# Key-query products of a linear attention: float32 products replaced by three rounded products of a split

## The reference, cut to what matters

```
phi(x) = exp(x @ omega.T - max(x @ omega.T)) / sqrt(128) + 1e-6        (128 features; the term in |x|^2 cancels)
qp, kp = phi(heads(x @ Wq)), phi(heads(x @ Wk));  v = heads(x @ Wv)
out[s] = sum_{t<=s} (qp[s] . kp[t]) v[t]  /  (sum_{t<=s} (qp[s] . kp[t]) + 1e-6)
```

## Time and profile before

| | |
|---|---|
| runs, us | 849.5, 846.65, 847.43; median 847.43 |
| profiled execution, us | 851.56 |
| its span, us | 849.6 |
| TensorE's mean granted clock, share of full | 0.987 |
| TensorE busy, us | 812.2 (96%) |
| VectorE busy, us | 617.9 (73%) |
| ScalarE busy, us | 428.7 (50%) |
| GpSimd busy, us | 401.4 (47%) |

### The profile page before, as it was taken

How to read it: one execution, slowest core, us unless ns; L and a number is a source line. 1 busy time by engine, 2 the same in 40 slices (tenths; PEclk the granted TensorE clock), 3 DMA queues, 4 the chain that set the end, 5 groups by cost and what they waited for, 6 DMA issues and landing times.

```text
span 849.6 us, 21134 instructions
## 1 busy us (share of the span) xinstructions
PE 812.2 (96%) x5921; PEld 760.3 (89%) x5922; DVE 617.9 (73%) x1770; ACT 428.7 (50%) x1184; POOL 401.4 (47%) x567
## 2 busy tenths in 40 slices
PE   6889999999999999999999999999989899999995
PEld 5778999999999999999999999999887799999994
DVE  4536787878888788878888888887776566666663
ACT  4335627365462735446372645627142366666663
POOL 5320233534526353452636245263435348787675
PEclk9889999999999999999999999999999999999998
DMA  9635936557483654738375574836499457777780
GB/s 266 213 119 196 309 104 226 180 185 271 140 277 112 237 200 162 268 132 286 97 253 181 181 252 145 288 109 231 168 426 364 149 102 130 123 127 127 115 135 3
DMA packets 105673, 161.19 MB, mean 190 GB/s; under 512 B 10672, under 2 KB 69616, under 8 KB 104752
## 3 DMA queue, kind: packets, MB, share of 16 engines
q1 hardware_dynamic: 79616, 115.62, 41.1%
q0 software_dynamic: 15792, 35.17, 17.1%
q10 hardware_dynamic: 10224, 9.89, 4.4%
HBM read 50.14 MB, written 112.47 MB: 191 GB/s over the span
## 4 chain that ended last, share of the span: by engine, by line
PE 87%; DVE 5%; issue 2%; POOL 2%; DMA 1%; ACT 1%; SPq 0%; POOLq 0%; DVEq 0%; ACTq 0%
PE ps L791 74%; PE ps L802 5%; PE ps L1016 3%; PE ps L1114 2%; PE ps L1136 2%; POOL rstd L605 1%; DVE stat L1434 1%; DVE xn L1445 1%; DMA raw_wT<-in_omegaT 1%; POOL expert_rows L676 0%; POOL veps L603 0%; DVE mv L1438 0%; DMA expert_rows<-relu_v,place_i 0%; DVE kpT L1664 0%; DVE fT_lo L1452 0%
## 5 line engine op out<-in xcount | busy, mean ns | idle before, releaser
L782 POOL DMA_INDIRECT out<-narrow,sidx x79 | 122.4, 1550 | 50.6 <-DVE sidx L1825 27.6
L616 POOL CAST ctx_hi<-ctx_raw 128x512 fp32r<-128x512 f32 x16 | 10.2, 639 | 191.1 <-DMA ctx_raw<-in_ctxT 188.5
L791 PE MATMUL ps<-w_hi,fT_hi 128*128 128x256 f32 x256 | 79.3, 310 | 1.4 <-DVE fT_lo L1452 1.4
L1238 ACT ACTIVATE phi<-ps,nmax 128x128 f32<-128x128 f32 x256 | 73.0, 375 | 5.5 <-DVE nmax L1573 5.4
L791 PE MATMUL ps<-hT_hi,w_hi 128*128 128x256 f32 x256 | 73.1, 286 | 1.5 <-DVE hT_lo L1452 1.5
L1187 ACT ACTIVATE xn3T<-ps 128x512 f32<-128x512 f32 x17 | 10.2, 599 | 124.5 <-PE ps L802 124.5
L791 PE MATMUL ps<-hT_hi,w_lo 128*128 128x256 f32 x256 | 72.4, 283 | 0.0
L791 PE MATMUL ps<-hT_lo,w_hi 128*128 128x256 f32 x256 | 72.4, 283 | 0.0
L791 PE MATMUL ps<-w_hi,fT_lo 128*128 128x256 f32 x256 | 72.2, 282 | 0.0
L791 PE MATMUL ps<-w_lo,fT_hi 128*128 128x256 f32 x256 | 72.1, 282 | 0.0
L1252 ACT ACTIVATE relu_v<-ps,b_sb 128x256 f32<-128x256 f32 x128 | 67.0, 523 | 0.0
(11 more groups left out here) (300 smaller groups left out, 2866.5 us busy)
## 6 DMA issues: line engine op xcount, KB each, us to landing
expert_rows<-zero_rows SPq DMA_DIRECT2D x16, 4352.0 KB, 14.6
narrow<-expert_rows ACTq DMA_DIRECT2D x71, 136.0 KB
expert_up_hi<-X SPq DMA_DIRECT2D x16, 352.0 KB, 2.8
e_lo<-expert_up_lo POOLq DMA_DIRECT2D x2, 2816.0 KB, 13.9
e_hi<-expert_up_hi POOLq DMA_DIRECT2D x2, 2816.0 KB, 22.5
part_raw<-in_E SPq DMA_DIRECT2D x30, 176.0 KB, 2.8
expert_up_lo<-part_raw SPq DMA_DIRECT2D x15, 352.0 KB, 3.1
X<-in_x SPq DMA_DIRECT2D x16, 256.0 KB, 2.8
```

The source lines that it names most:

```text
L782: pool.indirect_dma_start(out_rows, bass.IndirectOffsetOnAxis(sidx[:, u:u + 1], 0), yg[:, u, :], None, bounds_check=NT * P - 1, oob_is_err ...
L791: return pe.matmul(out_, lhsT, rhs, start=start, stop=stop)
L1238: last = act.activation(phi[:, g, h, :], ps[:, g, h * M:(h + 1) * M], ACT.Exp, bias=nmax[:, g, h:h + 1])
```

## The change

Key and query features become pairs like the other matrices. ScalarE now writes the rounded parts of both, `qpT` and `kpT`, without the scale and with an added 1e-6 x sqrt(128). VectorE writes the remainders, `qpT_lo` and `kpT_lo`, with one instruction of 1024 columns each, from PSUM and the rounded part; they lie in the memory of `phi`, where each head's `aT` now has 512 columns, so that it overwrites its own head's remainders. TensorE does `mm3` for both products of a head: six rounded products in place of two float32 ones. The scale, twice 1/sqrt(128), lies in the mask's ones. VectorE waits for all of the turned keys and for both of ScalarE's halves of each.

```diff
@@ -64,6 +64,7 @@
     NASSIGN = NT * P * TOPK
     SCORE_SCALE = float(D) ** -0.5
     PHI_SCALE = float(M) ** -0.5
+    EXP_EPS = FEAT_EPS / PHI_SCALE
     PROJ_SCALE = float(DH) ** -0.25
     V1W = DH + 1
     ATW = S + P
@@ -184,9 +185,11 @@
         X = sb1("X", [P, NT, D])
         wq, wk = (cut(pair(n, DC * H * M), "p (c n) -> p c n", c=DC) for n in ("wq", "wk"))
         wv, wo = (cut(pair(n, DC * D), "p (c n) -> p c n", c=DC) for n in ("wv", "wo"))
-        phi = sb1("phi", [P, 4, H, M])
-        qpT = sb1("qpT", [P, H, S])
-        kpT = sb1("kpT", [P, H, S])
+        with ExitStack() as phi_scope:
+            phi = sb1("phi", [P, 4, H, M], F32, phi_scope)
+        pT_lo = sb1("pT_lo", [P, H, 2 * S], F32R)
+        qpT = sb1("qpT", [P, H, S], F32R)
+        kpT = sb1("kpT", [P, H, S], F32R)
         xnT, attnT = (cut(pair(n, DC * S), "p (c s) -> p c s", c=DC) for n in ("xnT", "attnT"))
         attn_cols = 2 * (2 * DC * H * M + 2 * DC * D) + 4 * H * M + 2 * H * S + 4 * DC * S
         up_cols = NE * 2 * INTER
@@ -231,7 +234,9 @@
         assert TS * TOPK * RW <= 4 * S + TS * H * V1W
         rows_cross = xn_attn[:, :].rearrange("p (t j w) -> p t j w", t=TS, j=TOPK)
         rows_last = relu_v1[:, 0:TS * TOPK * RW].rearrange("p (t j w) -> p t j w", t=TS, j=TOPK)
-        aT = phi[:, :, :, :].rearrange("p g h m -> p (g h m)")[:, 0:H * ATW].rearrange("p (h s) -> p h s", h=H)
+        of_head = phi[:, :, :, :].rearrange("p g h m -> p (g h m)").rearrange("p (h w) -> p h w", h=H)
+        aT = of_head[:, :, 0:ATW]
+        qpT_lo, kpT_lo = (pT_lo[:, :, n * S:(n + 1) * S] for n in range(2))
         early_scope.close()
 
 
@@ -569,9 +574,9 @@
             pool.memset(halfneg[:, :], -0.5).then_inc(const_ready, 1)
             pool.memset(eps_ln[:, :], LN_EPS).then_inc(const_ready, 1)
             pool.memset(eps_attn[:, :], ATTN_LN_EPS).then_inc(const_ready, 1)
-            pool.memset(feat_eps[:, :], FEAT_EPS).then_inc(const_ready, 1)
+            pool.memset(feat_eps[:, :], EXP_EPS).then_inc(const_ready, 1)
             pool.memset(v1[:, :, :, DH:V1W], 1.0).then_inc(const_ready, 1)
-            pool.memset(mask[:, :], 1.0).then_inc(blank, 1)
+            pool.memset(mask[:, :], PHI_SCALE * PHI_SCALE).then_inc(blank, 1)
             pool.wait_ge(blank, 2)
             pool.affine_select(out=ident[:, :], in_=ones[:, :], compare_op=ALU.is_equal, fill=0.0, base=0,
                                pattern=[[-1, P]], channel_multiplier=1).then_inc(const_ready, 1)
@@ -1032,11 +1037,13 @@
                 if last_cross:
                     count_choices()
                 if a is not None:
-                    pe.wait_ge(qpT_ready, a + 1)
-                    pe.wait_ge(kpT_ready, a + 1)
+                    pe.wait_ge(qpT_ready, (a + 1) * 2)
+                    pe.wait_ge(kpT_ready, (a + 1) * 2)
                     for h in range(H):
-                        mm(ps[:, h, 0:S], kpT[:, h, 0:P], qpT[:, h, :])
-                        mm(ps[:, h, S:ATW], kpT[:, h, P:S], qpT[:, h, P:S]).then_inc(aT_ps, 1)
+                        for cols_out, keys, lo in ((slice(0, S), slice(0, P), 0), (slice(S, ATW), slice(P, S), P)):
+                            last = mm3(ps[:, h, cols_out], (kpT, kpT_lo), (qpT, qpT_lo), (slice(None), h, keys),
+                                       (slice(None), h, slice(lo, S)), True, True)
+                        last.then_inc(aT_ps, 1)
                 if f is not None and not last_ffn:
                     ffn_out(1, 2, FC // 2)
                 if a is not None:
@@ -1330,8 +1337,12 @@
                 if a is not None:
                     for n in range(2):
                         act.wait_ge(qpT_ps, a * 2 + (n + 1))
-                        last = act.activation(qpT[:, 2 * n:2 * n + 2, :], bank(n), ACT.Identity,
-                                              bias=feat_eps[:, 0:1], scale=PHI_SCALE)
+                        last = act.activation(qpT[:, 2 * n:2 * n + 2, :], bank(n), ACT.Identity, bias=feat_eps[:, 0:1])
+                    last.then_inc(qpT_ready, 1)
+                    for n in range(2):
+                        act.wait_ge(kpT_ps, a * 2 + (n + 1))
+                        last = act.activation(kpT[:, 2 * n:2 * n + 2, :], bank(2 + n), ACT.Identity,
+                                              bias=feat_eps[:, 0:1])
                     last.then_inc(qpT_ready, 1)
                 for p in splits_of(i):
                     hold(act, part_loaded, (i + 1) * (4 * 16))
@@ -1659,11 +1670,12 @@
                     dve.wait_ge(egap_ready, r + 1)
                     gates(r)
                 if a is not None:
-                    for n in range(2):
-                        dve.wait_ge(kpT_ps, a * 2 + (n + 1))
-                        last = dve.tensor_scalar(kpT[:, 2 * n:2 * n + 2, :], bank(2 + n), PHI_SCALE, FEAT_EPS,
-                                                 ALU.mult, ALU.add)
-                    last.then_inc(kpT_ready, 1)
+                    dve.wait_ge(kpT_ps, (a + 1) * 2)
+                    for n, (lo, hi) in enumerate(((qpT_lo, qpT[:, :, :]), (kpT_lo, kpT[:, :, :]))):
+                        dve.wait_ge(qpT_ready, a * 2 + (n + 1))
+                        whole = ps[:, 2 * n:2 * n + 2, :].rearrange("p n (h s) -> p (n h) s", h=2)
+                        dve.scalar_tensor_tensor(lo, whole, EXP_EPS, hi.bitcast(F32), ALU.add, ALU.subtract)\
+                            .then_inc(kpT_ready, 1)
                 if nxt is not None:
                     hold(dve, x_loaded, (nxt + 1) * 16)
                     ln_stats(0, nxt, lambda t: x_tile(nxt, t))
```

## The result

The changed kernel takes 876.61 us (median of 4 runs, 874.49 to 877.54) against 847.04 of the kernel before in the same comparison; the ratio is 1.0343, with an interval of 1.0318 to 1.0367. The forecast was slower, 865.6 us, range 857 to 884: the direction and the range held, but the cost is 29.6 us and not 18.2.

The account below looks back on a forecast made before the run. TensorE, busy 812.2 of 849.6 us, was taken as the bound, with VectorE's chain to xn3 level in five turns. 5 x 1.15 + 8 x 1.0 + 1.5 + 1.8 + 1.15 = 18.2 us on 847.43 gave 865.6, range 857 to 884.

Parts of the forecast that it names:

- The step that failed: Turns 0 and 1: longer waits for the features plus 0.34 us for the products, 1.5 and 1.8 us.
- (a): Rival: short rounded products no cheaper than float32 ones, 213 ns at 128 columns, 880 us; chance 0.27.
- (d): Rival: VectorE's remainders at 1.64 us, 0.8 us more in each turn, 878 us; chance 0.10.
- Steady turns: Turns 2 to 14: VectorE's delay to xn3 adds 1.15 us in five turns and 1.0 in eight.
- The five turns that waited for `xn3`: Turns where TensorE already waited 0.5 us for VectorE's normalised rows; VectorE's delay adds its full 1.15 us.
- TensorE's late start: Key-query products in turn 8 start at 334.47, 0.52 us late, behind VectorE's remainders.
- The products: 24 rounded key-query products per turn at 0.12 us each: 2.88 us, 0.34 longer than now.
- (b): Rival: split stays under the cover, only TensorE's saving is left, 10 us less, 837 us; chance 0.06.
- The remainders: VectorE's one instruction of 1024 elements each for q and k: 1.25 us, pitch 1.17, upper end 1.64.
- ScalarE's: ScalarE also does the two kpT halves; the 1.17 us move is covered by idle time and costs nothing.
- The last turn: No successor to normalise: 0.8 us for the start and 0.34 for the products, 1.15 us.

Follow-up runs that it names:

- e1_warm01: Changed kernel with needless matmuls filling TensorE's waits of turns 0 and 1: 865.83 us, ratio 1.0225.
- e7_before_warm: Kernel before with needless matmuls in TensorE's waits of turn 0: 847.96 us, ratio 1.0007.
- e6_two_stages_warm: Changed kernel, waits of turns 0 and 1 filled, first two products of heads 0 and 1 ahead of the wait for the keys' remainder: 865.43 us, ratio 1.0158.
- e2_warm0: Changed kernel with needless matmuls filling TensorE's waits of turn 0 only: 871.36 us, ratio 1.0279.
- e5_split_only: Changed kernel with remainders written but unused, two plain float32 products per head on the rounded parts: 869.74 us, ratio 1.0223.
- e3_before_late01: Kernel before with needless VectorE reductions ahead of kpT in turns 0 (two) and 1 (three): 855.26 us, ratio 1.0096.
- e4_products_only: Changed kernel without remainders, rounded parts standing in for them in the three products, evictions as before: 849.43 us, ratio 0.9993.

## Why the prediction was right, and where it was not

- **The step that failed** is the one for turns 0 and 1, "1.15 + 0.34 = 1.5" and "1.8". They measured 7.1 and 6.8 us. What was missing is a term: the clock. Filling the waits (e1_warm01) takes 6.1 and 5.1 us back and leaves 1.0 and 1.7. The rows of before had a sign of it: behind the 1.86 us wait of turn 0 the 16 float32 records took 4.24 us, behind no wait 2.78, for the clock was at the lower level from 29.0 to 32.4 us. The prediction never looked at the granted clock by stretch. That this low stretch grows long when rounded products follow the wait could not be read from the trace of before.
- **The number.** The range held, but by luck: its upper part was there for rivals (a) and (d), 880 and 878, and neither happened. That e1_warm01's 865.83 us is the forecast's 865.6 is in part luck too: the steady turns cost 1.1 us more than forecast and the last turn 1.15 less. The 1.0 us of its turn 0 is against a kernel before whose own clock fell there; against e7_before_warm, filled like it, it is 2.8 us, with 1.5 forecast, and where the other 1.3 lie is open.
- **Steady turns.** Forecast 13.75 us for the turns 2 to 14, measured 11.8 in the two traces and 14.9 with the slow `rstd` taken out of both. An ordinary turn from 5 on grew by 1.08 us (36.88 to 37.96), with 1.0 forecast, and the mechanism was right: VectorE's chain and not TensorE's late start sets it (e6_two_stages_warm). The turns 2, 3 and 4 differ: like with like they grew by 0.7, 2.0 and 1.4. The five turns that waited for `xn3` were read as a property of those turns, where they are those in which `rstd` was slow in that execution. On VectorE the delay of 1.3 us at the mask products shrinks to 1.0 at the statistics, since the four mask products waited for heads before (2.27 us) and run on without a wait now (1.94). TensorE's own delay of 0.67 + 0.23 us is nearly as long, and the wait appears ahead of the products and not, as forecast, at `xn3`.
- **TensorE's late start** was 0.67 us and not 0.52: VectorE started the first remainder 2.06 us after the transposes began (311.21 to 313.27), where 1.94 was assumed. Of the 0.15 us too little, 0.06 stood at the end of the second remainder (315.63), and 0.09 came because TensorE went on 0.14 us after it and not 0.05.
- **The products**: forecast 0.34 us longer, measured 0.23. In the head shown the six follow each other at 0.19, 0.12, 0.12, 0.06, 0.11 and 0.11 us: the first 128-column product is followed after 60 ns, the other two stand at the pace of the 65-column products, which suggests their weight loads. Rival (a), 213 ns, is out, and so is (b): streaming alone would have been 1.92 us. The Trainium skill (TensorE: Matmul & The Clock Gate, Back-to-back issue gap) has about 81 ns per matmul for a stream of loads and matmuls of 128 columns. The three 128-column products of the head shown have a mean of 93 ns (0.28 / 3), nearer to that than to the 0.12 us taken here. The 2.77 us of all 24 products is nearer to the 2.88 forecast than to the 2.41 estimated by that figure.
- **The remainders** took 1.22 us (forecast 1.25); rival (d) is out. **ScalarE's** added copies show no cost: in the steady turn shown its `kpT` is done at 314.28, ahead of VectorE's remainder at 314.41.
- **The last turn**, forecast 1.15 us: from its transposes to the end of the span 259.1 us after and 259.0 before. What follows it hid the delay.
- **The sum.** 1.5 + 1.8 + 13.75 + 1.15 = 18.2 was forecast. The traces have 7.1 + 6.8 + 11.8 - 0.5 = 25.2, and 28.3 with the steady turns like with like (14.9). The comparison of the medians has 29.6; the profiled execution of before was itself 4.5 us above its median, and its five slow `rstd` are 3.9 us of time.

## What to carry to other kernels

A wait has two prices: its length, and what TensorE's clock does after it. Read the granted clock stretch by stretch before costing a longer wait, above all where the pipeline fills, and ask what runs behind the wait. Splitting a float32 product into three rounded ones did not pay here, where each comes with its own weight load and the split itself lies on the chain that already holds the turn; moving work off one reader of a level chain only helps if the next reader has reserve. Before two traces are subtracted, see whether they are alike where the change does nothing: here five slow `rstd` against one hid 3 of 15 us. And see from the runs' times and mean clocks whether the traced execution is a usual one.

## What the runs showed of the hardware

- A wait of 1.89 us on TensorE was followed by 13.6 us at the lower clock level when rounded products came next (the traces of the changed kernel and of e2_warm0, turn 1), and by 3.4 us of it when float32 products of the same size came next (e5_split_only, turn 1); a wait of 2.55 us with float32 products had 3.4 us too (e3_before_late01). What in the products makes the difference was not tried.
- It differs from execution to execution: behind a wait of 1.79 us and with rounded products (e4_products_only, turn 0) the traced execution was at the lower level from 29.0 to 56.3 us, and by their mean clocks only three of ten runs were like it.
- The level falls without a wait too: in the kernel before at 39.2 us, among 16 products of one column that follow each other.
- At the full level 24 rounded products of 256 and 128 columns took 2.77 us, 16 float32 records of the same sizes 2.54: three rounded products are no cheaper than one float32 product at these sizes.
- One instruction of VectorE over 1024 columns from PSUM takes 1.22 us; two over 512 took 1.26 and 1.28.
- GpSimd's `rstd` (a power operation over 128x2 elements) takes 0.74 us in most turns and 1.54 in some, and the turn is 0.7 to 0.8 us longer where it does. How many turns have it changes from execution to execution (0 to 9 of 13 in the table); why stays open. A long turn (8) and a short one (5) of the kernel before:

```profile
338.86 1.54 POOL L605 TENSOR_TENSOR rstd<-veps,halfneg 128x2 f32<-128x2 f32 x1
...
227.44 0.74 POOL L605 TENSOR_TENSOR rstd<-veps,halfneg 128x2 f32<-128x2 f32 x1
```
